# Two normalisations of a recurrence moved from VectorE to GpSimd, with one more pipeline stage and statistics kept for two tiles

## The chip, the cores and the metric

The kernel runs on one core of one Trainium2 chip. The core has TensorE (PE in the profile; its weight loads are PEld), VectorE (DVE), ScalarE (ACT), GpSimd (POOL) and SyncE (SP), which here issues DMAs. The metric is the time of one execution in device microseconds; lower is better.

## The reference

The input x is 2 x 1024 x 128 in float32. With `ln` a layer norm without gain, the program computes

```
x = x + 0.5 * F(ln(x))          # F: 6 layers of windowed attention and gated MLP
x = x + R(ln(x))                # R: a linear recurrence over time
x = x + 0.5 * F(ln(x))          # the same weights again

R(u):  h = u @ w_in.T + b_in
       s_t = sigmoid(a) * s_(t-1) + b * h_t      # per channel, along the 1024 positions
       return s @ w_out.T + b_out
```

Each layer of F projects to 16 heads of 64, normalises and rotates queries and keys, attends within windows of 32 and the window before, projects back and adds, then applies a gated MLP with a hidden width of 341. The change lies wholly in the middle: R, and the two layer norms around it.

## The kernel before, in words

The sequence is cut into 16 tiles of 128 positions (8 for each of the two sequences). 12 layers (6, and the same 6 again) times 16 tiles make 192 tile-layers. All engines run one software pipeline over them, fully unrolled: in step `s`, the stage with lag `L` works on tile-layer `s - L`. The stages of F have the lags 0 (transpose the input, project), 1 (keys, values, scores), 2 (softmax), 4 (attention output), 5 and 6 (MLP). Within a step, the order of each engine's instructions is simply the order of the code in its `step` function; engines meet at semaphores. The names used here:

- `proj`, `tps`, `sps`, `ops` are PSUM tensors that PE writes. `rot` (128x2048) holds rotated queries and keys, `swp` the other half of the rotation, `prob` the softmax, `hT` the hidden MLP values that PE multiplies at the end.
- `Z` holds the running activations of F, `xb` the residual x.

R is worked in between as further stages, active only for the 16 tiles between the 6th and the 7th layer. Their lags are named `M_...` and count from step 80 on:

- `M_X` = 7: DVE adds 0.5 Z to `xb` (L923), takes statistics (L938), aggregates them to mean and variance in `mmv[:, 0]` (L957) and adds the epsilon into `mrs` (L963). GpSimd raises that to the power -0.5 (L1138).
- `M_NORM` = 8: DVE normalises the tile into `mx_n` (L948), GpSimd adds the output bias `boB` to `xb` (L1142).
- `M_T` = 9: PE transposes `mx_n` (L650), ScalarE copies it out.
- `M_IN` = 10: PE multiplies by `winT` (L623), DVE adds bias and gain (L918) and runs the scan along time (L932, two inputs in SBUF: `siga` broadcast, and `mbh`).
- `M_OUT` = 11: PE multiplies by `woutT` (L626), DVE adds the result to `xb` (L914), takes its statistics (L928), aggregates (L953), adds the epsilon (L960); GpSimd takes the power (L1138).
- `M_Z` = 12: DVE normalises the tile into `Z` (L942), which the 7th layer reads: SP shifts it by DMA from stage 0 of tile-layer 96 on.

In DVE's `step`, `middle(k)` stands behind the last instruction of the reciprocal root (`rn`, L882) and ahead of `hT` (L1037), the row maximum `mx` (L1044) and the subtraction of it (L1047). On GpSimd a step is: a power on `rt` (L1114, the MLP's norm), the division of `prob` (L1118), two additions into `rot` (L1124), a small product for the tables (L1098), two multiplications of `rot` by `rn` (L1133, 128x1024 each, which wait for L882), then the middle's powers and the bias. A full step is one in which all these middle stages are active, a plain step one in which none is.

Of the kernel before, what the change touches and what calls it, by code (L numbers as in the profile page):

```python
# [17 lines left out]
ALU = mybir.AluOpType  # L18
# [3 lines left out]
P = 128  # L22
# [4 lines left out]
POS = SEQ // P  # L27
# [16 lines left out]


L_X, L_QKV, L_S, L_SM, L_AV, L_WO, L_F, L_F2 = 0, 1, 2, 3, 4, 4, 5, 6
M_X, M_NORM, M_T, M_IN, M_OUT, M_Z = 7, 8, 9, 10, 11, 12
FRONT = 6
UNROLL = 2
MID, MID_END = N - TILES + M_X - 1, N + M_Z  # L50
# [6 lines left out]
def macaron(nc, x_in, w_in, b_in, a_in, b_gain, w_out, b_out, w_qkv, q_scale, k_scale, w_o,  # L57
            ln_g, ln_b, w_1, b_1, w_2, b_2, c_rope, c_mask, c_ident, out):
    with ExitStack() as ctx:
# [7 lines left out]
        Z = sb("Z", [SLOTS * P])  # L67
# [47 lines left out]
        rawT = sb("rawT", [RAW])  # L115
        siga = sb("siga", [1])
        mst = sb("mst", [2, 6])
        mmv = sb("mmv", [2, 2])
        mrs = sb("mrs", [2])
        mx_n = sb("mx_n", [P])  # L120
        mx_t = sb("mx_t", [P])
        mbh = sb("mbh", [P])
# [694 lines left out]
        def _(dve):  # L817
# [90 lines left out]
            def middle(k):  # L908

                t = k.mid(M_OUT)  # L910
                if t is not None:
                    k.wait(p_f2, L_F2)
                    k.wait_mid(m_bo, M_OUT)
                    v.tensor_tensor(xb[:, t, :], xb[:, t, :], ops[:, 1, P:2 * P], ALU.add).then_inc(m_x2, 1)  # L914
                t = k.mid(M_IN)
                if t is not None:
                    k.wait(p_f2, L_F2)
                    v.tensor_scalar(mbh[:, :], ops[:, 1, 0:P], rawT[:, RAW_C:RAW_C + 1], rawT[:, RAW_C + 2:RAW_C + 3],  # L918
                                    ALU.add, ALU.mult).then_inc(m_bh, 1)
                t = k.mid(M_X)  # L920
                if t is not None:
                    k.wait(v_z, L_F2 + 1, base=TILES)
                    v.scalar_tensor_tensor(out=xb[:, t, :], in0=zslot(t), scalar=0.5, in1=xb[:, t, :],  # L923
                                           op0=ALU.mult, op1=ALU.add).then_inc(m_x1, 1)
                t = k.mid(M_OUT)
                if t is not None:
                    k.wait_mid(m_x2, M_OUT)
                    v.bn_stats(mst[:, 1, :], xb[:, t, :]).then_inc(m_st2, 1)  # L928
                t = k.mid(M_IN)
                if t is not None:  # L930
                    k.wait_mid(m_bh, M_IN)
                    v.tensor_tensor_scan(ys[:, t % 2, :], siga[:, :].to_broadcast([P, P]), mbh[:, :],  # L932
                                         0.0 if t % POS == 0 else ys[:, 1 - t % 2, P - 1:P],
                                         ALU.mult, ALU.add).then_inc(m_y, 1)
                t = k.mid(M_X)
                if t is not None:
                    k.wait_mid(m_x1, M_X)
                    v.bn_stats(mst[:, 0, :], xb[:, t, :]).then_inc(m_st, 1)  # L938
                t = k.mid(M_Z)
                if t is not None:  # L940
                    k.wait_mid(m_rs2, M_Z)
                    v.tensor_scalar(zslot(t), xb[:, t, :], mmv[:, 1, 0:1], mrs[:, 1:2],  # L942
                                    ALU.subtract, ALU.mult).then_inc(m_z, 1)
                t = k.mid(M_NORM)
                if t is not None:
                    k.wait(p_xT, L_X)
                    k.wait_mid(m_rs, M_NORM)
                    v.tensor_scalar(mx_n[:, :], xb[:, t, :], mmv[:, 0, 0:1], mrs[:, 0:1],  # L948
                                    ALU.subtract, ALU.mult).then_inc(m_xn, 1)
                if k.mid(M_OUT) is not None:  # L950
                    k.wait_mid(m_st2, M_OUT)
                    k.wait_mid(m_z, M_OUT + 1)
                    v.bn_aggr(mmv[:, 1, :], mst[:, 1, :]).then_inc(m_ag2, 1)  # L953
                if k.mid(M_X) is not None:
                    k.wait_mid(m_st, M_X)
                    k.wait_mid(m_xn, M_X + 1)
                    v.bn_aggr(mmv[:, 0, :], mst[:, 0, :]).then_inc(m_ag, 1)  # L957
                if k.mid(M_OUT) is not None:
                    k.wait_mid(m_ag2, M_OUT)
                    v.tensor_scalar(mrs[:, 1:2], mmv[:, 1, 1:2], 1e-5, None, ALU.add).then_inc(m_ve2, 1)  # L960
                if k.mid(M_X) is not None:
                    k.wait_mid(m_ag, M_X)
                    v.tensor_scalar(mrs[:, 0:1], mmv[:, 0, 1:2], 1e-5, None, ALU.add).then_inc(m_ve, 1)  # L963

            def step(k):
                if k.on(L_QKV):
# [126 lines left out]
        def _(pool):  # L1093
# [16 lines left out]
            def step(k):  # L1110
                if k.on(L_F):
                    k.wait(v_ve, L_F)
                    k.wait(a_xn, L_F + 1)
                    g_.tensor_tensor(rt2[:, 1:2], rt2[:, 0:1], half[:, 0:1], ALU.pow).then_inc(g_rstd, 1)  # L1114
                if k.on(L_SM):
                    k.wait(v_rec, L_SM)
                    pr = prob[:, :, :, :].rearrange("p a t j -> p (a t) j")
                    g_.tensor_tensor(pr, pr, rr[:, :].unsqueeze(2).to_broadcast([P, HEADS, 2 * WIN]),  # L1118
                                     ALU.mult).then_inc(g_nrm, 1)
                if k.on(L_QKV):  # L1120
                    for g in range(2):
                        k.wait(v_ab[1 + g], L_QKV)
                        r = rot[:, g * INNER:(g + 1) * INNER]
                        g_.tensor_tensor(r, r, swp[:, g * INNER:(g + 1) * INNER], ALU.add).then_inc(g_add[g], 1)  # L1124
                    src = k.off("rsrc", L_QKV, lambda u: (u % TILES) * (2 * DH))
                    dst = k.off("rdst", L_QKV, lambda u: ((u + TILES) % (2 * TILES)) * (2 * DH))
                    sc = k.off("rscl", L_QKV, lambda u: ((u // 4) % (4 * DEPTH)) * DH + 4 * DH)
                    tables(src, dst, sc)
                    k.wait(v_rs, L_QKV, per=RS_STEPS)
                    for g in range(2):  # L1130
                        k.wait(g_add[g], L_QKV)
                        r = heads(rot[:, g * INNER:(g + 1) * INNER])
                        g_.tensor_tensor(r, r, rn[:, g * HEADS:(g + 1) * HEADS].unsqueeze(2)  # L1133
                                         .to_broadcast([P, HEADS, DH]), ALU.mult).then_inc(g_nm[g], 1)
                for lag, n, ve, done in ((M_OUT, 1, m_ve2, m_rs2), (M_X, 0, m_ve, m_rs)):
                    if k.mid(lag) is not None:
                        k.wait_mid(ve, lag)
                        g_.tensor_tensor(mrs[:, n:n + 1], mrs[:, n:n + 1], half[:, 0:1], ALU.pow).then_inc(done, 1)  # L1138
                t = k.mid(M_NORM)
                if t is not None:  # L1140
                    k.wait_mid(m_xn, M_NORM)
                    g_.tensor_tensor(xb[:, t, :], xb[:, t, :], boB[:, :], ALU.add).then_inc(m_bo, 1)  # L1142

            def outer_pow(g):
                first, end = GROUPS[g]
# [87 lines left out]
```

## Time and profile before

| | |
|---|---|
| median of 3 runs | 3404.82 us (3398.56 to 3405.36) |
| the profiled execution, its own time | 3406.23 us |
| its span in the profile | 3404.4 us |
| mean granted TensorE clock | 0.992 |
| busy PE, DVE, ACT, POOL | 97%, 82%, 71%, 65% |
| shortest and longest L948 (128x128) | 1.673 and 2.012 us |
| shortest and longest L942 (128x128) | 0.331 and 1.857 us |

A busy time counts an instruction from its recorded start to its recorded end, so an instruction that is held by something after its start counts as busy. In the timeline, starts of neighbouring instructions on one engine can lie a little before the end of the one ahead. An idle time is put down to the instruction that ended it.

### The profile page before, as it was taken

The numbers are of one execution on the slowest core, as the hardware profiler recorded it, in microseconds if no ns is written. First come the engines' busy times: TensorE is split into PE (matmuls) and PEld (weight loads), VectorE is DVE, ScalarE is ACT, GpSimd is POOL, SyncE is SP. The second block draws the span as 40 slices with busy tenths as digits, with TensorE's granted clock in tenths as the row PEclk, the third lists the DMA queues.
The fourth block names the chain that finished last, engine by engine and source line by source line (L and its number), as shares of the span: only waits on it lengthen the run. The fifth ranks groups of instructions, "written<-read, shape, count | busy, mean of one in ns | idle before, by whom it ended". The sixth has DMA issues, their size and how long they took to land. (4 is left out here: it accounts for less than half of the span.)

```text
span 3404.4 us, 150755 instructions
## 1 busy us (share of the span) xinstructions
PE 3289.8 (97%) x63324; PEld 2485.3 (73%) x63515; DVE 2794.2 (82%) x6984; ACT 2426.8 (71%) x3769; POOL 2202.1 (65%) x1422
## 2 busy tenths in 40 slices
PE   6999999999999999999999999999999999999998
PEld 4777777777777777777667777777777777777776
DVE  5888888888888888889999888888888888888885
ACT  2777777777777777777667777777777777777775
POOL 4666666666666666666666666666666666666663
PEclk7999999999999999999999999999999999999998
DMA  3111111111111111111111111111111111111111
GB/s 114 51 47 51 48 51 48 50 48 47 51 47 51 48 50 48 51 48 45 46 41 46 51 48 51 48 51 44 48 48 51 48 51 48 51 48 50 50 51 42
DMA packets 199180, 170.06 MB, mean 50 GB/s; under 512 B 139610, under 2 KB 172525, under 8 KB 198509
## 3 DMA queue, kind: packets, MB, share of 16 engines
q1 hardware_dynamic: 193901, 157.05, 16.9%
q8 instruction: 509, 8.34, 1.0%
q10 hardware_dynamic: 4608, 3.34, 0.3%
q14 instruction: 162, 1.33, 0.1%
HBM read 33.38 MB, written 1.05 MB: 10 GB/s over the span
## 5 line engine op out<-in xcount | busy, mean ns | idle before, releaser
L1124 POOL TENSOR_TENSOR rot<-rot,swp 128x1024 f32<-128x1024 f32 x384 | 907.2, 2362 | 142.0 <-DVE rot L901 142.0
L705 ACT ACTIVATE sq<-proj 128x512 f32<-128x512 f32 x768 | 437.8, 596 | 573.5 <-PE proj L503 564.0
L503 PE MATMUL proj<-wq,xsT 128*128 128x512 f32 x1536 | 778.7, 627 | 30.0 <-DVE hT L1037 16.7
L1133 POOL TENSOR_TENSOR rot<-rot,rn 128x1024 f32<-128x1024 f32 x384 | 724.0, 1906 | 0.0
L1114 POOL TENSOR_TENSOR rt<-rt,half 128x1 f32<-128x1 f32 x192 | 105.3, 548 | 848.2 <-DVE rt L983 848.2
L895 DVE TENSOR_TENSOR swp<-proj,tab 128x512 f32<-128x512 f32 x768 | 522.1, 680 | 17.8 <-ACT sq L705 15.7
L901 DVE TENSOR_TENSOR rot<-proj,tab 128x512 f32<-128x512 f32 x768 | 519.0, 676 | 1.8 <-PE tps L514 1.8
L514 PEld LDWEIGHTS tps<-idf,rot 128*128 128x128 f32 x3072 | 361.6, 141 | 207.7 <-issue 203.5
L1037 DVE SCALAR_TENSOR_TENSOR hT<-proj,b1c,fg 114x128 f32<-114x128 f32 (+1 forms) x576 | 166.6, 345 | 413.5 <-ACT fg L769 407.3
L1118 POOL TENSOR_TENSOR prob<-prob,rr 128x1024 f32<-128x1024 f32 x192 | 365.4, 1903 | 187.3 <-DVE rr L995 187.3
L540 PEld LDWEIGHTS sps<-kT,qT 64*32 64x32 f32 x24576 | 365.5, 106 | 131.3 <-issue 130.9
L503 PEld LDWEIGHTS proj<-wq,xsT 128*128 128x128 f32 x1536 | 259.5, 190 | 255.4 <-issue 136.6
L540 PE MATMUL sps<-kT,qT 64*32 64x64 f32 x24576 | 407.5, 217 | 38.8 <-issue 38.7
L514 PE MATMUL tps<-idf,rot 128*128 128x128 f32 x3072 | 400.8, 274 | 3.2 <-POOL rot L1133 2.3
L509 PE MATMUL proj<-wq,xsT 128*128 128x512 f32 x768 | 386.1, 597 | 2.5 <-DVE rot L901 2.2
L555 PE MATMUL ops<-pT,vb 64*64 64x32 f32 x12288 | 378.8, 220 | 2.1 <-issue 2.1
L555 PE MATMUL ops<-pT,va 64*64 64x32 f32 x12288 | 375.8, 219 | 3.1 <-issue 2.9
L606 PE MATMUL ops<-wo,oT 128*128 128x128 f32 x3072 | 376.4, 276 | 2.4 <-ACT oT L727 2.4
L606 PEld LDWEIGHTS ops<-wo,oT 128*128 128x128 f32 x3072 | 359.8, 193 | 2.6 <-issue 2.6
L555 PEld LDWEIGHTS ops<-pT,vb 64*64 64x64 f32 x12288 | 329.4, 134 | 35.4 <-issue 34.7
L555 PEld LDWEIGHTS ops<-pT,va 64*64 64x64 f32 x12288 | 331.1, 135 | 4.0 <-issue 3.9
L522 PEld LDWEIGHTS proj<-xnT,w 128*114 128x114 f32 (+1 forms) x2304 | 264.3, 178 | 87.1 <-issue 81.7
(113 smaller groups left out, 5687.4 us busy)
## 6 DMA issues: line engine op xcount, KB each, us to landing
vb<-va SPq DMA_DIRECT2D x192, 384.0 KB, 3.5
vb<-va SPq DMA_DIRECT2D x192, 128.0 KB, 3.4
wq<-in_L_ffn_Wqkv SPq DMA_DIRECT2D x95, 192.0 KB
xs<-Z SPq DMA_DIRECT2D x384, 32.0 KB
xs<-Z SPq DMA_DIRECT2D x384, 28.0 KB
xs<-Z SPq DMA_DIRECT2D x384, 3.8 KB
xs<-Z SPq DMA_DIRECT2D x384, 0.2 KB
wo<-in_L_ffn_Wo SPq DMA_DIRECT2D x94, 64.0 KB
```

The lines of the kernel that those rows point to most:

```text
L503: mm(proj[:, c % 2, :], xsT[:, k.parity(L_QKV), :], wq2[:, bass.ds(w + c * 512, 512)], start=True, stop=True).then_inc(p_qkv[c], 1)
L509: mm(proj[:, c, :], xsT[:, k.parity(L_S), :], wq2[:, bass.ds(w + (4 + c) * 512, 512)], start=True, stop=True).then_inc(p_v[c], 1)
L514: last = tr(tps[:, p, :], rot[:, g * INNER + p * P:g * INNER + (p + 1) * P], idf[:, :])
L540: last = mm(sps[to:to + WIN, ty, p * 64:p * 64 + 64], qT[rows, p, w * WIN:(w + 1) * WIN], kT[rows, p, at:at + 2 * WIN], start=False, stop= ...
L555: last = mm(o4[hp * DH:(hp + 1) * DH, g, :], v, pT[rows, p, to:to + WIN], start=True, stop=True, skip_group_check=True)
L606: last = mm(ops[:, 0, 0:P], oT[:, p, :], wo[:, bass.ds(w + p * P, P)], start=(p == 0), stop=(p == PAIRS - 1))
L705: fn(sq[:, c * 512:(c + 1) * 512], proj[:, c % 2, :], ACT.Square).then_inc(a_sq[c], 1)
L895: v.tensor_tensor(halves(swp[:, c * 512:(c + 1) * 512]), swapped, tab[:, bass.ds(po + (2 * g + 1) * POS * DH, DH)] .rearrange("p (a d) -> ...
L901: v.tensor_tensor(heads(rot[:, c * 512:(c + 1) * 512]), heads(src), tab[:, bass.ds(po + 2 * g * POS * DH, DH)].unsqueeze(1) .to_broadcast( ...
L1118: g_.tensor_tensor(pr, pr, rr[:, :].unsqueeze(2).to_broadcast([P, HEADS, 2 * WIN]), ALU.mult).then_inc(g_nrm, 1)
L1124: g_.tensor_tensor(r, r, swp[:, g * INNER:(g + 1) * INNER], ALU.add).then_inc(g_add[g], 1)
L1133: g_.tensor_tensor(r, r, rn[:, g * HEADS:(g + 1) * HEADS].unsqueeze(2) .to_broadcast([P, HEADS, DH]), ALU.mult).then_inc(g_nm[g], 1)
```

## The change

- `M_Z` and `M_NORM` run on GpSimd, in a function `middle(k)` at the end of its step, behind the multiplications of `rot`.
- A new stage `M_ST` = 8 takes the statistics of the tile that `M_X` = 7 wrote a step before. `M_NORM`, `M_T`, `M_IN`, `M_OUT`, `M_Z` become 9, 10, 11, 12, 13.
- `mmv` and `mrs` have two slots, by the parity of the tile, so an aggregation waits for the reader of two tiles ago.
- On DVE, the statistics of `M_ST` stand ahead of those of `M_OUT`, and both ahead of the scan; before, the statistics of `M_X` stood behind it.
- The addition of `boB` goes from `M_NORM` to `M_T`; it and the two powers stand behind the two normalisations on GpSimd.

```diff
-M_X, M_NORM, M_T, M_IN, M_OUT, M_Z = 7, 8, 9, 10, 11, 12
+M_X, M_ST, M_NORM, M_T, M_IN, M_OUT, M_Z = 7, 8, 9, 10, 11, 12, 13
...
-        mmv = sb("mmv", [2, 2])
-        mrs = sb("mrs", [2])
+        mmv = sb("mmv", [2, 2, 2])
+        mrs = sb("mrs", [2, 2])
...
+                t = k.mid(M_ST)
+                if t is not None:
+                    k.wait_mid(m_x1, M_ST)
+                    v.bn_stats(mst[:, 0, :], xb[:, t, :]).then_inc(m_st, 1)
                 t = k.mid(M_OUT)
                 if t is not None:
                     k.wait_mid(m_x2, M_OUT)
...
-                t = k.mid(M_X)
-                if t is not None:
-                    k.wait_mid(m_x1, M_X)
-                    v.bn_stats(mst[:, 0, :], xb[:, t, :]).then_inc(m_st, 1)
-                t = k.mid(M_Z)
-                if t is not None:
-                    k.wait_mid(m_rs2, M_Z)
-                    v.tensor_scalar(zslot(t), xb[:, t, :], mmv[:, 1, 0:1], mrs[:, 1:2],
-                                    ALU.subtract, ALU.mult).then_inc(m_z, 1)
-                t = k.mid(M_NORM)
-                if t is not None:
-                    k.wait(p_xT, L_X)
-                    k.wait_mid(m_rs, M_NORM)
-                    v.tensor_scalar(mx_n[:, :], xb[:, t, :], mmv[:, 0, 0:1], mrs[:, 0:1],
-                                    ALU.subtract, ALU.mult).then_inc(m_xn, 1)
...
+                for n, lag, st_done, read, ag in ((0, M_ST, m_st, (m_xn, M_ST + 2), m_ag),
+                                                  (1, M_OUT, m_st2, (m_z, M_OUT + 2), m_ag2)):
+                    t = k.mid(lag)
+                    if t is not None:
+                        k.wait_mid(st_done, lag)
+                        k.wait_mid(*read)
+                        v.bn_aggr(mmv[:, n, t % 2, :], mst[:, n, :]).then_inc(ag, 1)
...
+            def middle(k):
+
+                t = k.mid(M_Z)
+                if t is not None:
+                    k.wait_mid(m_rs2, M_Z)
+                    g_.tensor_scalar(zslot(t), xb[:, t, :], mmv[:, 1, t % 2, 0:1], mrs[:, 1, t % 2:t % 2 + 1],
+                                     ALU.subtract, ALU.mult).then_inc(m_z, 1)
                 t = k.mid(M_NORM)
                 if t is not None:
-                    k.wait_mid(m_xn, M_NORM)
+                    k.wait(p_xT, L_X)
+                    k.wait_mid(m_rs, M_NORM)
+                    g_.tensor_scalar(mx_n[:, :], xb[:, t, :], mmv[:, 0, t % 2, 0:1], mrs[:, 0, t % 2:t % 2 + 1],
+                                     ALU.subtract, ALU.mult).then_inc(m_xn, 1)
+                t = k.mid(M_T)
+                if t is not None:
+                    k.wait_mid(m_xn, M_T)
                     g_.tensor_tensor(xb[:, t, :], xb[:, t, :], boB[:, :], ALU.add).then_inc(m_bo, 1)
```

On DVE a full step reads, between `rn` and `mx`, before (line, operation, output<-inputs, shape; the scan L932 is listed as SCALAR_TENSOR_TENSOR):

```order
L914 TENSOR_TENSOR xb<-xb,ops 128x128
L918 TENSOR_SCALAR mbh<-ops,rawT 128x128
L923 SCALAR_TENSOR_TENSOR xb<-Z,xb 128x128
L928 BN_STATS mst<-xb 128x6
L932 SCALAR_TENSOR_TENSOR ys<-siga,ys,mbh 128x128
L938 BN_STATS mst<-xb 128x6
L942 TENSOR_SCALAR Z<-xb,mmv,mrs 128x128
L948 TENSOR_SCALAR mx_n<-xb,mmv,mrs 128x128
L953 BN_AGGR mmv<-mst 128x2
L957 BN_AGGR mmv<-mst 128x2
L960 TENSOR_SCALAR mrs<-mmv 128x1
L963 TENSOR_SCALAR mrs<-mmv 128x1
```

and now (the scan is L936):

```order
L914 TENSOR_TENSOR xb<-xb,ops 128x128
L918 TENSOR_SCALAR mbh<-ops,rawT 128x128
L923 SCALAR_TENSOR_TENSOR xb<-Z,xb 128x128
L928 BN_STATS mst<-xb 128x6
L932 BN_STATS mst<-xb 128x6
L936 SCALAR_TENSOR_TENSOR ys<-siga,ys,mbh 128x128
L945 BN_AGGR mmv<-mst 128x2 x2
L950 TENSOR_SCALAR mrs<-mmv 128x1 x2
```

The two normalisations are gone, and the scan has moved behind the second statistics instruction.

On GpSimd a full step reads before, from the small table product on:

```order
L1098 TENSOR_TENSOR tab<-rope,scl 128x128
L1133 TENSOR_TENSOR rot<-rot,rn 128x1024 x2
L1138 TENSOR_TENSOR mrs<-mrs,half 128x1 x2
L1142 TENSOR_TENSOR xb<-xb,boB 128x128
L1114 TENSOR_TENSOR rt<-rt,half 128x1
```

and now:

```order
L1086 TENSOR_TENSOR tab<-rope,scl 128x128
L1121 TENSOR_TENSOR rot<-rot,rn 128x1024 x2
L1133 TENSOR_SCALAR Z<-xb,mmv,mrs 128x128
L1139 TENSOR_SCALAR mx_n<-xb,mmv,mrs 128x128
L1144 TENSOR_TENSOR xb<-xb,boB 128x128
L1150 TENSOR_TENSOR mrs<-mrs,half 128x1 x2
L1102 TENSOR_TENSOR rt<-rt,half 128x1
```

Two instructions of 128x128 have come in behind the multiplications of `rot`, and the powers went behind the bias.

## Rows read from the trace of the kernel before

**Rows 1.** The page's first part: busy us (share of the span) and instructions.

```profile
PE 3289.8 (97%) x63324; PEld 2485.3 (73%) x63515; DVE 2794.2 (82%) x6984; ACT 2426.8 (71%) x3769; POOL 2202.1 (65%) x1422
```

**Rows 2.** Windows: stretch, length; PE, PEld, DVE, ACT, POOL busy (instructions); clock; DMA.

```profile
1314.94:1520.28 205.34, 202.25 (x3949) 153.35 (x3962) 169.34 (x424) 151.25 (x234) 135.69 (x85) 1.00 0.18 49
1520.28:1590.72 70.44, 69.74 (x1327) 52.08 (x1331) 69.25 (x168) 50.93 (x81) 49.14 (x36) 1.00 0.18 48
1590.72:1805.50 214.78, 196.10 (x3675) 146.23 (x3685) 212.75 (x518) 141.31 (x227) 143.53 (x113) 1.00 0.16 44
1805.50:1825.14 19.64, 17.95 (x334) 13.29 (x335) 19.12 (x44) 12.58 (x20) 13.03 (x11) 1.00 0.13 36
1825.14:1860.36 35.22, 34.87 (x667) 26.48 (x669) 34.60 (x86) 24.79 (x39) 22.73 (x15) 1.00 0.18 48
1860.36:1894.59 34.23, 33.90 (x660) 25.70 (x662) 29.76 (x78) 25.21 (x39) 22.99 (x17) 1.00 0.18 49
```

**Rows 3.** Waits (total us, times, longest): two of the plain stretch, one of the full.

```profile
DVE hT L1037 <- ACT fg L769: 26.6, 12, 2.4
PE sps L540 <- issue: 2.5, 5, 1.0
...
PE proj L503 <- DVE hT L1037: 14.4, 10, 1.8
```

**Rows 4.** Timeline of DVE, a full step: start, duration, line, operation.

```profile
1648.51 0.87 DVE L1037 SCALAR_TENSOR_TENSOR hT<-proj,b1c,fg 114x128 f32<-114x128 f32 x3
...
1663.29 0.28 DVE L928 BATCH_NORM_STATS2 mst<-xb 128x6 f32<-128x128 f32 x1
1663.49 0.47 DVE L932 TENSOR_TENSOR_SCAN ys<-siga,ys,mbh 128x128 f32<-128x128 f32 x1
1663.88 0.26 DVE L938 BATCH_NORM_STATS2 mst<-xb 128x6 f32<-128x128 f32 x1
1664.07 1.67 DVE L942 TENSOR_SCALAR Z<-xb,mmv,mrs 128x128 f32<-128x128 f32 x1
1665.66 1.94 DVE L948 TENSOR_SCALAR mx_n<-xb,mmv,mrs 128x128 f32<-128x128 f32 x1
1667.52 0.17 DVE L953 BATCH_NORM_AGGREGATE mmv<-mst 128x2 f32<-128x6 f32 x1
...
1668.04 0.87 DVE L1037 SCALAR_TENSOR_TENSOR hT<-proj,b1c,fg 114x128 f32<-114x128 f32 x3
```

**Rows 5.** Timeline of POOL in the same step.

```profile
1654.56 0.55 POOL L1114 TENSOR_TENSOR rt<-rt,half 128x1 f32<-128x1 f32 x1 [4.59 <-DVE rt L983]
...
1663.18 0.50 POOL L1098 TENSOR_TENSOR tab<-rope,scl 128x128 f32<-128x128 f32 x1
1663.64 3.87 POOL L1133 TENSOR_TENSOR rot<-rot,rn 128x1024 f32<-128x1024 f32 x2
1668.00 1.06 POOL L1138 TENSOR_TENSOR mrs<-mrs,half 128x1 f32<-128x1 f32 x2 [0.48 <-DVE mrs L960]
1669.04 0.45 POOL L1142 TENSOR_TENSOR xb<-xb,boB 128x128 f32<-128x128 f32 x1
```

**Rows 6.** Timeline of DVE at the start: the first normalisation, with GpSimd idle.

```profile
4.64 0.35 DVE L837 TENSOR_SCALAR Z<-xb,mvo,rstd 128x128 f32<-128x128 f32 x1 [0.74 <-POOL rstd L1148]
```

**Rows 7.** Timelines of DVE and POOL in a step without scan, second of the recurrence.

```profile
1534.62 2.01 DVE L948 TENSOR_SCALAR mx_n<-xb,mmv,mrs 128x128 f32<-128x128 f32 x1
1536.95 0.15 DVE L963 TENSOR_SCALAR mrs<-mmv 128x1 f32<-128x1 f32 x1
...
1534.65 3.76 POOL L1133 TENSOR_TENSOR rot<-rot,rn 128x1024 f32<-128x1024 f32 x2
```

**Rows 8.** Timeline of PE in the full step: the recurrence's transposition and the next.

```profile
1661.91 0.27 PE L650 MATMUL tps<-idf,mx_n 128*128 128x128 f32 x1
1662.02 0.27 PE L652 MATMUL tps<-idf,xs 128*128 128x128 f32 x1
```

More of the change, by code:

```diff
@@ L944, in middle @@
-                t = k.mid(M_NORM)
-                if t is not None:
-                    k.wait(p_xT, L_X)
-                    k.wait_mid(m_rs, M_NORM)
-                    v.tensor_scalar(mx_n[:, :], xb[:, t, :], mmv[:, 0, 0:1], mrs[:, 0:1],
-                                    ALU.subtract, ALU.mult).then_inc(m_xn, 1)
[L950 to L963, printed above, removed]
+                for n, lag, st_done, read, ag in ((0, M_ST, m_st, (m_xn, M_ST + 2), m_ag),
[5 more added lines that the diff above has]
+                        v.bn_aggr(mmv[:, n, t % 2, :], mst[:, n, :]).then_inc(ag, 1)
@@ L965, in step @@
+                for n, lag, ag, ve in ((0, M_ST, m_ag, m_ve), (1, M_OUT, m_ag2, m_ve2)):
+                    t = k.mid(lag)
+                    if t is not None:
+                        k.wait_mid(ag, lag)
+                        v.tensor_scalar(mrs[:, n, t % 2:t % 2 + 1], mmv[:, n, t % 2, 1:2], 1e-5, None,
+                                        ALU.add).then_inc(ve, 1)
             def step(k):
@@ L1134, in step, with zslot @@
                                          .to_broadcast([P, HEADS, DH]), ALU.mult).then_inc(g_nm[g], 1)
[L1135 to L1138, printed above, removed]
+                middle(k)
+            def zslot(t):
+                return Z[:, (t + t // POS + 1) * P:(t + t // POS + 2) * P]
+            def middle(k):
[4 more added lines that the diff above has]
+                                     ALU.subtract, ALU.mult).then_inc(m_z, 1)
                 t = k.mid(M_NORM)
                 if t is not None:
-                    k.wait_mid(m_xn, M_NORM)
-                    g_.tensor_tensor(xb[:, t, :], xb[:, t, :], boB[:, :], ALU.add).then_inc(m_bo, 1)
+                    k.wait(p_xT, L_X)
[3 more added lines that the diff above has]
+                t = k.mid(M_T)
+                if t is not None:
+                    k.wait_mid(m_xn, M_T)
+                    g_.tensor_tensor(xb[:, t, :], xb[:, t, :], boB[:, :], ALU.add).then_inc(m_bo, 1)
+                for lag, n, ve, done in ((M_OUT, 1, m_ve2, m_rs2), (M_ST, 0, m_ve, m_rs)):
+                    t = k.mid(lag)
+                    if t is not None:
+                        k.wait_mid(ve, lag)
+                        r = mrs[:, n, t % 2:t % 2 + 1]
+                        g_.tensor_tensor(r, r, half[:, 0:1], ALU.pow).then_inc(done, 1)
             def outer_pow(g):
```

## The prediction

> **What bounds the kernel now.** I read the page's summary first. TensorE (PE) is busy 97% of the span, VectorE (DVE) 82%, GpSimd (POOL) 65% [rows 1]. That says "PE", but it is an average over nearly 200 steps of one software pipeline, and the change touches only some 20 steps in the middle. So the second view is the table of stretches, cut where the row maximum (`mx`, L1044) of successive steps starts [rows 2]. Twelve plain steps take 205.34 us, 17.11 each. The 11 steps in which every part of the recurrence is active take 214.78 us, 19.53 each. In the plain stretch DVE is busy 169.34 of 205.34 us; in the full one 212.75 of 214.78. The recurrence's steps are bound by DVE, and PE has slack there.
>
> The waits say the same [rows 3]. In plain steps DVE sits before `hT` for ScalarE's `fg` (26.6 us in 12 steps); in full steps DVE never waits for an engine and PE waits for `hT` (14.4 us over 10 recorded waits, up to 1.8 each). Plain steps also hold irregular PE pauses of up to 1.0 us without a releaser (5 in 12 steps), part of the 17.11.
>
> Then one full step in the timeline [rows 4, 5]. Two DVE instructions stick out: the normalisation into `Z` (L942, 1.67 us) and the one into `mx_n` (L948, 1.94 us). The same work takes 0.35 us at the start of the kernel when GpSimd is idle [rows 6]. Their ends tell why they are long: GpSimd's two multiplications of `rot` (L1133) run from 1663.64 to 1667.51, half each, so the first ends near 1665.5 and the second at 1667.51. L942 ends at 1665.74, L948 at 1667.60. Each was held until the GpSimd instruction beside it was done. Nearly all of their 3.61 us is waiting for GpSimd, not work.
>
> **What the change removes.** L942 and L948 leave DVE. From L942's start (1664.07) to L953's start (1667.52) is 3.45 us per full step [rows 4]. If nothing took their place, DVE's step would be 19.53 - 3.45 = 16.08, less than PE needs. PE's own need is 17.11 plus the recurrence's five matmul instructions (two for each of the two projections, one transposition), at 0.11 each, the spacing of L650 and L652 [rows 8]: 17.66.
>
> **What it moves, and why the gain is smaller on DVE.** The new order puts the statistics of `x1` ahead of those of `x2`, and both ahead of the scan. The scan therefore starts one statistics instruction later, 0.20 us (L928 to L932, 1663.29 to 1663.49) [rows 4]. That matters. Does a scan contend with GpSimd? The rows say so from GpSimd's side: in the step with the scan the two multiplications take 3.87 us [rows 5], in one without it 3.76 [rows 7]; the scan, which starts 0.15 us ahead of them while the table product L1098 still runs, gets in between and costs them 0.11. Against that, L948 in the early step starts at 1534.62, 0.03 ahead of the multiplication at 1534.65, and is held the whole 2.01 us [rows 7]. So the race is lost somewhere between 0.15 and 0.03 us of lead. The moved scan would start at 1663.69, 0.05 *behind* the multiplication at 1663.64. I expect it to be held until the first multiplication ends.
>
> The Trainium skill (SBUF — State Buffer, "Who interferes with whom") has the same rule: a VectorE instruction with two SBUF inputs contends with a GpSimd instruction that reads SBUF, and the loser blocks for the whole instruction. By that rule the scan blocks; 3.87 against 3.76 agrees.
>
> Worked out for a full step: the second multiplication would start at 1663.64 + 1.88 = 1665.52. The scan today ends 0.32 us after a multiplication's start (1663.96 against 1663.64), so it would end at 1665.84 and the next instruction start 0.08 earlier, as L938 does, at 1665.76. From L953 to `hT` is 0.52 (1667.52 to 1668.04), so `hT` starts at 1666.28. The last `hT` was at 1648.51: a step of 17.77 us, against 19.53. That is just above PE's 17.66, so either engine's irregular pauses are now partly seen; I add 0.13 and take 17.9.
>
> The small instructions that follow (two aggregations, two additions of one element) now run while the second multiplication does. Are they held? No: L963 took 0.15 us at 1536.95, inside GpSimd's 1534.65 to 1538.41 [rows 7], and 0.15 when GpSimd was idle. They stay at nothing.
>
> **What it adds on GpSimd.** Two 128x128 `tensor_scalar` per full step. The trace has none on GpSimd. Nearest by size is the 128x128 addition L1142, 0.45 us; above it the 128x1024 multiplication, 1.9 us for eight times the elements [rows 5]; below nothing is not to be had. I take 0.45 each. Do they hide? GpSimd's next step begins with the power of `rt` (L1114), which it awaits from DVE: at 1654.56, 6.05 us behind the `hT` at 1648.51. In the new step the multiplications start 2.64 us ahead of `hT` and take 3.87; then come 2c for the two new ones, 0.45 and 1.06 (L1142, L1138). GpSimd is free at 2.74 + 2c behind `hT`, against 6.05: c may be 1.65 us before anyone waits. At 0.45 there is 2.4 us to spare; at 1.9 it is missed by 0.5, some 5 us in all. The second new instruction also brings a wait to GpSimd, for PE's transposition of `xs` (L652): that started at 1662.02, over 5 us before GpSimd gets there, so the powers queued behind it lose nothing.
>
> **The added stage and the double statistics** cost no step: the pipeline's length stays. They give each result a step of distance. The DMA queue (SP) issues nothing new; it waits for `z` of a tile at the step L_X, four steps behind the old writing and three behind the new one. On GpSimd the addition of `boB` and the two powers now stand behind the normalisations; PE's transposition and DVE's additions want them a step later. The statistics move off the value written just ahead of them, worth a few hundredths of a microsecond beside other waits. All taken as nothing.
>
> **The sum** by stretches [rows 2]:
> - first four steps, 70.44 us (one held normalisation in each): new 4 x 17.11 plus PE's extras of 0.44 = 68.88, -1.6
> - 11 full steps, 214.78: new 11 x 17.9 = 196.9, -17.9
> - the step at 1805.50, 19.64: the scan is 0.28 earlier without `x1`'s addition and wins its race, new 17.66, -2.0
> - the next two, 35.22, now PE-bound at 17.66: +0.1
> - the last two, 34.23, with one stage more still active: 17.55 + 17.33, +0.65
>
> Together -20.7, say -21. The profiled execution took 3406.2 us (its span 3404.4): 3385. It lies 1.4 above the median of the runs shown, 3404.8, so the median should be 3384.
>
> **The rivals.**
> - *The scan is not held* (the race is won, or lost by less): DVE's step is 16.1 and PE bounds at 17.66. Full steps give -20.6, in all -23.4; where the irregular pauses vanish too, 0.2 to 0.3 a step more, -27. About 3381, down to 3378. For it: the race is within 0.1 us. Against: L948. Chance 0.15.
> - *The hold passes on in full*: the scan, once held, is not let in between the two multiplications but behind both. Then it ends near 1667.7, the step is about 19.6 and only the edges gain: -2, 3403. The Trainium skill (Perfetto Trace Analysis, "Optimizing Scalar/DVE Operations") warns that since GpSimd and VectorE share a port, offloading between them might not help; this would be that case. Against it: L942 did get in between in every full step. Chance 0.08.
> - *GpSimd becomes the bound* (the slower side): each new instruction costs c, more than 1.65, and the step becomes 17.77 + 2c - 3.3. The gain of a full step is gone at c = 2.5. At c = 3, half more than the 128x1024 multiplication, it is 20.5, 0.95 longer than before in the 10 steps that hold both, 0.8 and 2.7 longer in the two behind them, with -1.6 from the first of the 11 full steps (only one of the two runs there) and -0.9 from the edges left: +10.5, 3415. For it: no such instruction in the trace, and operands given per partition. Against: 3 is nearly seven times the 128x128 row. Chance 0.03.
> - The forecast keeps 0.74.
>
> The Trainium skill (GPSIMD Engine Reference, "Instruction dispatch") gives about 6 us for the first call of a freshly loaded GpSimd kernel. By it the sum would be some 4 us smaller, once; the trace shows no such gap where GpSimd changes from copies to products.
>
> **How the numbers follow.** A measurement of this kernel tells about 0.2% from no change, 6.8 us. Faster by more: the forecast, the first rival, nearly all: 0.90. Within, mainly the second rival: 0.07. Slower: 0.03. The range reaches below to the first rival's 3378, above to GpSimd at its upper bound (+5, 3389), and 3 and 5 us beyond, because the three runs shown lie 7 us apart: 3375 to 3394. The second and third rival stay outside.
>
> **What would show it.** Steps of 17.6 to 18.0 us from the first full step on. A scan (L936) of about 2.1 us in 11 steps that ends 0.3 behind the first multiplication's end, 0.5 to 0.7 in the others. `hT` still not waiting for ScalarE in full steps. PE's wait for `hT` down from 1.8 to a few tenths. GpSimd's new instructions near 0.45 us, with 2 to 3 us of idle time ahead of the power that begins its next step. Scans of 0.5 us everywhere would be the first rival; steps of 19.5 with scans of 4 us the second; GpSimd without idle time ahead of the power the third.

## The result and the profile after

Over four runs each, the changed kernel takes 3377.97 us in the median (3377.11 to 3380.69) and the one before 3401.69 us (3397.75 to 3405.36): a ratio of 0.9925, with a 95% interval of 0.9913 to 0.9938. It is 24 us faster. The forecast was 3384, the range 3375 to 3394. Two executions of experiments, of 8,369 and 11,475 us on one chip, are left out below; in the one of them that was profiled, TensorE was slow throughout (a projection instruction, L503, took 1,411 ns in the mean, against 627 in the kernel before).

The page's first part of the changed kernel, against [rows 1]:

```profile
PE 3288.9 (97%) x63515; PEld 2482.8 (73%) x63515; DVE 2758.7 (82%) x6952; ACT 2424.5 (72%) x3769; POOL 2227.0 (66%) x1454
```

VectorE has lost 35.5 us of busy time, GpSimd has gained 24.9. The span fell by 25.5 us (3404.4 to 3378.9). The windows of the changed kernel, cut at the same steps as [rows 2] (first four of the recurrence, 11 full ones, one, two, two; columns as there):

```profile
1521.26:1589.58 68.32, 67.75 (x1325) 51.67 (x1326) 61.51 (x158) 50.71 (x80) 48.36 (x35) 1.00 0.18 49
1589.58:1785.36 195.78, 191.88 (x3686) 146.56 (x3686) 192.11 (x495) 140.57 (x226) 157.82 (x130) 1.00 0.18 48
1785.36:1802.57 17.21, 17.13 (x335) 13.19 (x335) 15.66 (x44) 12.56 (x20) 13.77 (x13) 1.00 0.16 42
1802.57:1837.91 35.34, 34.99 (x671) 26.97 (x672) 31.21 (x83) 25.53 (x41) 28.57 (x24) 1.00 0.18 48
1837.91:1873.05 35.14, 34.60 (x667) 26.34 (x668) 30.37 (x81) 25.19 (x39) 25.29 (x20) 1.00 0.18 48
```

The 11 full steps went from 214.78 to 195.78 us, 19.53 to 17.80 each. The 20 steps together went from 374.31 to 351.79, 22.5 us less; the other 3.0 of the 25.5 lie outside them, nearly all of it code that has not changed.

A full step of the changed kernel in VectorE's timeline, against [rows 4]:

```profile
1638.98 0.27 DVE L932 BATCH_NORM_STATS2 mst<-xb 128x6 f32<-128x128 f32 x1
1639.18 2.13 DVE L936 TENSOR_TENSOR_SCAN ys<-siga,ys,mbh 128x128 f32<-128x128 f32 x1
1641.23 0.21 DVE L945 BATCH_NORM_AGGREGATE mmv<-mst 128x2 f32<-128x6 f32 x2
1641.42 0.22 DVE L950 TENSOR_SCALAR mrs<-mmv 128x1 f32<-128x1 f32 x2
1641.60 0.87 DVE L1025 SCALAR_TENSOR_TENSOR hT<-proj,b1c,fg 114x128 f32<-114x128 f32 x3
```

and in GpSimd's, against [rows 5]:

```profile
1639.13 3.87 POOL L1121 TENSOR_TENSOR rot<-rot,rn 128x1024 f32<-128x1024 f32 x2
1643.00 0.79 POOL L1133 TENSOR_SCALAR Z<-xb,mmv,mrs 128x128 f32<-128x128 f32 x1
1643.78 0.79 POOL L1139 TENSOR_SCALAR mx_n<-xb,mmv,mrs 128x128 f32<-128x128 f32 x1
1644.54 0.46 POOL L1144 TENSOR_TENSOR xb<-xb,boB 128x128 f32<-128x128 f32 x1
1644.95 1.08 POOL L1150 TENSOR_TENSOR mrs<-mrs,half 128x1 f32<-128x1 f32 x2
1647.65 0.55 POOL L1102 TENSOR_TENSOR rt<-rt,half 128x1 f32<-128x1 f32 x1 [1.62 <-DVE rt L971]
```

The reader is to see three things. The scan starts 0.05 us behind the multiplication (1639.18 against 1639.13) and takes 2.13 us instead of 0.47; this happens in all 11 full steps, from 1603.98 to 1781.88, and in none of the five others that have a scan, where it starts 0.15 to 0.38 ahead of the multiplication and takes 0.47 to 0.71. A normalisation on GpSimd costs 0.79 us, not 0.45. And there is still idle time (1.62 us) ahead of the power that opens GpSimd's next step.

The waits in the full steps changed with that. Waits of TensorE's weight loads for `hT` (total us, times, longest) before (1590.72 to 1805.50), and then in the changed kernel (1589.58 to 1785.36):

```profile
PEld proj L503 <- DVE hT L1037: 23.3, 11, 2.7
...
PEld proj L503 <- DVE hT L1025: 3.3, 8, 0.7
```

TensorE's matmuls no longer wait for `hT` there at all, and VectorE waits for another engine in two of the 11 steps only, for the scores (1.5 us together): it still sets the step in most of them.

### The profile page after: what moved, and what is told of

Same layout as the page of the kernel before. It is cut to its first block and busy times, and to the rows that moved or that the text cites. A ratio compares the mean times of both kernels' runs of the same rounds, so it can differ in the third digit from the quotient of the medians.

```text
span 3378.9 us, 150942 instructions
## 1 busy us (share of the span) xinstructions
PE 3288.9 (97%) x63515; PEld 2482.8 (73%) x63515; DVE 2758.7 (82%) x6952; ACT 2424.5 (72%) x3769; POOL 2227.0 (66%) x1454
## 3 DMA queue, kind: packets, MB, share of 16 engines
q14 instruction: 162, 1.33, 0.1%
## 5 line engine op out<-in xcount | busy, mean ns | idle before, releaser
L503 PE MATMUL proj<-wq,xsT 128*128 128x512 f32 x1536 | 772.4, 625 | 14.4 <-DVE rot L901 10.2
L503 PEld LDWEIGHTS proj<-wq,xsT 128*128 128x128 f32 x1536 | 261.0, 190 | 232.3 <-issue 139.3
L1032 DVE TENSOR_REDUCE mx<-sps 128x16 f32<-128x1024 f32 x192 | 235.1, 1224 | 114.7 <-PE sps L540 111.0
## 6 DMA issues: line engine op xcount, KB each, us to landing
vb<-va SPq DMA_DIRECT2D x192, 384.0 KB, 3.5
```

The lines of the kernel that those rows point to most:

```text
L503: mm(proj[:, c % 2, :], xsT[:, k.parity(L_QKV), :], wq2[:, bass.ds(w + c * 512, 512)], start=True, stop=True).then_inc(p_qkv[c], 1)
```

## The experiments

Each kernel was run beside the kernel before on the same chip. Scan first, no stage, late on VectorE and on VectorE shared one chip (the kernel before: 3401.5 us in the median). The other seven ran on another chip, in two groups: move only, twice and three times (before: 3398.9), and the four marked "again" (before: 3403.5). So rows of different groups are compared by their ratios. The table gives, from each kernel's profiled execution, the mean of the 11 full steps and the sum of the 22 steps from the first with `M_X` to the last with `M_Z` of the longer pipeline. The full steps are the last 11 in which both `M_X` and the output stage (`M_OUT`) run, cut at `mx` as in [rows 2]; with the old lags a twelfth lies ahead of them and is not counted.

| kernel | median us (n) | ratio to before, 95% | full step, us | 22 steps, us | rest of the span, us |
|---|---|---|---|---|---|
| before | 3401.7 (4) | | 19.53 | 408.7 | 2995.7 |
| changed | 3378.0 (4) | 0.9925 (0.9913 to 0.9938) | 17.80 | 386.6 | 2992.3 |
| changed, again | 3379.8 (5) | 0.9931 (0.9920 to 0.9943) | 17.75 | 386.7 | 2992.0 |
| scan first | 3375.7 (5) | 0.9921 (0.9907 to 0.9936) | 17.44 | 383.4 | 2989.2 |
| scan first, again | 3376.0 (5) | 0.9920 (0.9908 to 0.9932) | 17.50 | 384.0 | 2990.2 |
| no stage | 3381.1 (4) | 0.9935 (0.9922 to 0.9949) | 17.63 | 384.8 | 2994.8 |
| no stage, again | 3379.9 (5) | 0.9926 (0.9913 to 0.9939) | 17.58 | 383.5 | 2994.6 |
| late on VectorE | 3380.0 (4) | 0.9931 (0.9918 to 0.9945) | - | - | - |
| late on VectorE, again | 3382.0 (6) | 0.9940 (0.9926 to 0.9954) | 17.82 | 386.4 | 2993.4 |
| on VectorE | 3409.0 (11) | 1.0018 (1.0009 to 1.0026) | 19.85 | 415.5 | 2988.9 |
| move only | 3447.2 (4) | 1.0134 (1.0118 to 1.0151) | 21.87 | 460.0 | 2987.5 |
| twice | 3375.1 (4) | 0.9929 (0.9915 to 0.9944) | 17.71 | 386.0 | 2992.6 |
| three times | 3386.5 (4) | 0.9962 (0.9948 to 0.9977) | 18.49 | 396.8 | 2987.6 |

The last column is code that no kernel changes. It moves by 8 us between the profiled executions of different kernels, so times of whole kernels that lie 3 or 4 us apart say little unless they are measured side by side, and the steps say more. In the three kernels that were profiled twice it came out alike, within 0.3, 1.0 and 0.2 us. Whether it moves by chance or goes with the kernel is therefore open.

### The scan ahead of the statistics

```diff
...
-                t = k.mid(M_ST)
-                if t is not None:
-                    k.wait_mid(m_x1, M_ST)
-                    v.bn_stats(mst[:, 0, :], xb[:, t, :]).then_inc(m_st, 1)
                 t = k.mid(M_OUT)
...
                                          0.0 if t % POS == 0 else ys[:, 1 - t % 2, P - 1:P],
                                          ALU.mult, ALU.add).then_inc(m_y, 1)
+                t = k.mid(M_ST)
+                if t is not None:
+                    k.wait_mid(m_x1, M_ST)
+                    v.bn_stats(mst[:, 0, :], xb[:, t, :]).then_inc(m_st, 1)
```

> The changed kernel, with one edit: the scan stands ahead of the statistics of M_ST again, so that it starts about 0.2 us earlier. Theory A (the scan loses a race by 0.05 us and is then held by the first multiplication): the scan takes 0.47 us in all 11 full steps instead of 2.13, VectorE's full step shrinks to about 16 us, and TensorE sets the step: 17.35 us in a step without a pause (16.80 + 5 x 0.11), 17.66 in the mean with pauses. The changed kernel's full steps are 17.80 in the mean, so the gain is small: 1.5 us (0 to 5), about 3376 us. Theory B (VectorE is still the one bound of the full steps): the whole 1.7 us of the hold comes off each of 11 steps, 18 us, 3360.

Measured: 3375.7 us. Timelines of a full step (from the repetition below), VectorE and then GpSimd:

```profile
1635.58 0.47 DVE L932 TENSOR_TENSOR_SCAN ys<-siga,ys,mbh 128x128 f32<-128x128 f32 x1
1635.97 0.26 DVE L938 BATCH_NORM_STATS2 mst<-xb 128x6 f32<-128x128 f32 x1
...
1637.50 0.87 DVE L1025 SCALAR_TENSOR_TENSOR hT<-proj,b1c,fg 114x128 f32<-114x128 f32 x3 [0.58 <-ACT fg L769]
1638.65 1.23 DVE L1032 TENSOR_REDUCE mx<-sps 128x16 f32<-128x1024 f32 x1 [0.28 <-PE sps L540]
...
1635.73 3.88 POOL L1121 TENSOR_TENSOR rot<-rot,rn 128x1024 f32<-128x1024 f32 x2
```

0.15 us ahead of the multiplication instead of 0.05 behind it, the scan takes 0.47 us. That shows the race. VectorE's waits in the full steps (total us, times, longest), first of the changed kernel, then of this one:

```profile
DVE mx L1032 <- PE sps L540: 1.5, 2, 0.9
...
DVE hT L1025 <- ACT fg L769: 7.6, 11, 0.8
DVE mx L1032 <- PE sps L540: 4.9, 10, 1.4
```

VectorE now waits in every full step, for ScalarE and mostly for the scores too, as in a plain one: it is no longer the bound. So only a little of the 1.66 us per scan came off the time, as theory A says. The shortest full steps are 17.17 us, below the 17.35 I had worked out. The expectation for theory B, 3360 us, is far off.

The same pair side by side:

> The changed kernel once more, on the chip of the next three runs. On record it is 22.0 us shorter in the 22 steps of the recurrence and 3.5 us outside them, where nothing changed. Theory A (the 3.5 us are TensorE's irregular pauses, which fall differently in each execution): the median is 3375 to 3382 us, and the middle of the profiled execution is 22 us (21 to 24) shorter than before's.

> The changed kernel with the scan ahead of the statistics of M_ST, measured beside the changed kernel itself. The first look gave full steps of 17.44 us in the mean against 17.80, 4.0 us over 11 of them. Theory A: 3 to 5 us faster than the changed kernel on the same chip. Rival (TensorE's pauses swallow it): within 1.5 us.

3379.8 us (3378.3 to 3381.5) against 3376.0 (3374.7 to 3378.0): 3.8 us, and the runs do not overlap. Of that, 2.8 us lie in the 11 full steps (195.30 against 192.48 us). Theory A holds for both; the middle of the changed kernel is 22.0 us shorter than before's again. The reason given for the 3.5 us outside it, pauses that fall differently in each execution, is not borne out: that part is 2992.0 us, as it was (2992.3).

### The same normalisations on VectorE, where GpSimd is idle

Against the kernel before, besides the slots:

```diff
-                t = k.mid(M_Z)
-                if t is not None:
-                    k.wait_mid(m_rs2, M_Z)
-                    v.tensor_scalar(zslot(t), xb[:, t, :], mmv[:, 1, 0:1], mrs[:, 1:2],
-                                    ALU.subtract, ALU.mult).then_inc(m_z, 1)
...
                 if k.on(L_WO):
                     k.wait(d_xs2, L_WO, per=64)
                     v.bn_stats(st[:, :], xs2[:, :]).then_inc(v_bn, 1)
+                t = k.mid(M_Z)
+                if t is not None:
+                    k.wait_mid(m_rs2, M_Z)
+                    v.tensor_scalar(zslot(t), xb[:, t, :], mmv[:, 1, t % 2, 0:1], mrs[:, 1, t % 2:t % 2 + 1],
+                                    ALU.subtract, ALU.mult).then_inc(m_z, 1)
...
```

and the same for `M_NORM` and `mx_n`.

> The kernel before, with the two normalisations still on VectorE, but at the end of its step (behind the statistics st of the MLP's norm), where GpSimd is idle, and mmv and mrs in two slots. Old lags, scan where it was. Theory A (each normalisation costs 0.35 us and the rest was the hold by GpSimd's multiplication): both take 0.33 to 0.40 us, VectorE's full step is 16.7 us, TensorE sets it at 17.4 to 17.7, and the time is 3376 us, like the changed kernel, with no work moved to another engine. Rival (the instructions are long because of their per-partition operands, or VectorE simply has too much work): they stay above 1 us each, full steps stay near 19 us, 3395 or more.

Four executions gave a median of 3380.0 us; the fifth, the profiled one, is the one of 8,369 us. The same kernel again:

> The normalisations on VectorE at the end of its step, where GpSimd is idle; in the first attempt the profiled execution was unusable, because TensorE ran at a fraction of its speed in all of it. Theory A: both instructions take 0.33 to 0.40 us, full steps of 17.2 us without a pause, 17.4 to 17.7 in the mean, and the time is that of the kernel with the scan first, within 3 us. Rival: they stay above 1 us each.

Timelines of a full step of the repetition, VectorE and GpSimd:

```profile
1645.87 0.33 DVE L1044 TENSOR_SCALAR Z<-xb,mmv,mrs 128x128 f32<-128x128 f32 x1
1646.11 0.34 DVE L1050 TENSOR_SCALAR mx_n<-xb,mmv,mrs 128x128 f32<-128x128 f32 x1
...
1640.65 3.88 POOL L1132 TENSOR_TENSOR rot<-rot,rn 128x1024 f32<-128x1024 f32 x2
1644.49 1.06 POOL L1139 TENSOR_TENSOR mrs<-mrs,half 128x1 f32<-128x1 f32 x2
```

Over all tiles they take 0.329 to 0.345 us. The same instructions on the same engine took 1.67 and 1.94 us while GpSimd multiplied. This settles what the long durations were, and 21 us of the gain are to be had without moving any work to another engine. The second slots are in this kernel too; whether it needs them was not run. The time missed its expectation: it is 6 us above the kernel with the scan first, not within 3. Of these, 3.5 us are in the full steps, 17.82 us in the mean and not below 17.37. In the first full step (18.13 us) the scan starts 0.31 us behind the multiplication and takes 1.92 us. For the rest, the waits of TensorE's weight loads in the full steps point to a cause, first this kernel's, then that of the scan first, again (total us, times, longest):

```profile
PEld proj L503 <- DVE rot L901: 8.1, 12, 1.0
```

```profile
PEld proj L503 <- DVE rot L901: 2.8, 11, 0.3
```

The place at the end of VectorE's step lies directly ahead of the rotations, which TensorE's next projection waits for. By these waits 0.5 us of work there is late for TensorE. That is argued; no run moves the two instructions elsewhere in VectorE's idle stretch.

### The stage and the slots without the other engine

The changed kernel with both normalisations back in VectorE's `middle`, behind the scan:

```diff
                                          ALU.mult, ALU.add).then_inc(m_y, 1)
+                t = k.mid(M_Z)
+                if t is not None:
+                    k.wait_mid(m_rs2, M_Z)
+                    v.tensor_scalar(zslot(t), xb[:, t, :], mmv[:, 1, t % 2, 0:1], mrs[:, 1, t % 2:t % 2 + 1],
+                                    ALU.subtract, ALU.mult).then_inc(m_z, 1)
...
-                    g_.tensor_scalar(zslot(t), xb[:, t, :], mmv[:, 1, t % 2, 0:1], mrs[:, 1, t % 2:t % 2 + 1],
-                                     ALU.subtract, ALU.mult).then_inc(m_z, 1)
...
```

> The changed kernel with its stage, lags, slots and order, but the two normalisations back on VectorE, behind the scan. Theory A: three instructions contend now. The scan is held until the first multiplication ends, the normalisation into Z until the second ends, the one into mx_n perhaps behind GpSimd's addition of the bias: full steps of 19.5 to 20.0 us, 3400 to 3409 us, no gain over the kernel before. Rival (the stage and the two slots bring the gain, not the other engine): full steps near 17.8, 3378.

Measured: 3409.0 us, ratio 1.0018. Timelines of a full step, VectorE and GpSimd:

```profile
1643.22 1.72 DVE L936 TENSOR_TENSOR_SCAN ys<-siga,ys,mbh 128x128 f32<-128x128 f32 x1
1644.87 1.86 DVE L942 TENSOR_SCALAR Z<-xb,mmv,mrs 128x128 f32<-128x128 f32 x1
1646.64 0.49 DVE L948 TENSOR_SCALAR mx_n<-xb,mmv,mrs 128x128 f32<-128x128 f32 x1
...
1642.70 3.94 POOL L1132 TENSOR_TENSOR rot<-rot,rn 128x1024 f32<-128x1024 f32 x2
1646.60 0.45 POOL L1144 TENSOR_TENSOR xb<-xb,boB 128x128 f32<-128x128 f32 x1
```

The scan ends 0.3 us behind the middle of the multiplications (1644.94), the normalisation into `Z` at their end (1646.73 against 1646.64), and the one into `mx_n` is held a little by the bias: nine of the 11 full steps are 19.8 us long. Theory A; the stage and the slots by themselves bring nothing here. The steps are 0.3 us longer than before: the moved scan is held now (1.7 to 2.1 us), and with it a third instruction contends.

### The move without the second slot

Against the kernel before, with `mmv` and `mrs` as they were; the same for `mx_n`:

```diff
-                    v.tensor_scalar(zslot(t), xb[:, t, :], mmv[:, 1, 0:1], mrs[:, 1:2],
-                                    ALU.subtract, ALU.mult).then_inc(m_z, 1)
...
+                t = k.mid(M_Z)
+                if t is not None:
+                    k.wait_mid(m_rs2, M_Z)
+                    g_.tensor_scalar(zslot(t), xb[:, t, :], mmv[:, 1, 0:1], mrs[:, 1:2],
+                                    ALU.subtract, ALU.mult).then_inc(m_z, 1)
...
                 for lag, n, ve, done in ((M_OUT, 1, m_ve2, m_rs2), (M_X, 0, m_ve, m_rs)):
```

> The kernel before, with the two normalisations moved to GpSimd and nothing else: one slot of statistics, old lags. VectorE's aggregations now wait in the same step for GpSimd's normalisations (m_z, m_xn), which stand behind the two multiplications. Theory A (two slots are what makes the move pay): hT follows the second multiplication by 2 x 0.79 + 0.45 us, 1.5 later than before, full steps of 21 us; steps with one normalisation lose 2 to 2.6 us each; 35 us in all, 3437 us (3420 to 3445). Rival (the slots cost and bring nothing): 3378.

Measured: 3447.2 us, 48 us slower than before, and 2 us above the upper end of what was expected. VectorE and GpSimd in a full step:

```profile
1616.10 0.26 DVE L938 BATCH_NORM_STATS2 mst<-xb 128x6 f32<-128x128 f32 x1
1618.76 0.18 DVE L942 BATCH_NORM_AGGREGATE mmv<-mst 128x2 f32<-128x6 f32 x1 [2.40 <-POOL Z L1127]
1619.54 0.18 DVE L946 BATCH_NORM_AGGREGATE mmv<-mst 128x2 f32<-128x6 f32 x1 [0.60 <-POOL mx_n L1133]
...
1617.86 0.80 POOL L1127 TENSOR_SCALAR Z<-xb,mmv,mrs 128x128 f32<-128x128 f32 x1
1618.64 0.79 POOL L1133 TENSOR_SCALAR mx_n<-xb,mmv,mrs 128x128 f32<-128x128 f32 x1
```

The hold has become a semaphore wait, and it is longer: with one slot, VectorE may not aggregate before GpSimd has read the last statistics. The shortest full step is 21.00 us, as expected. So the slots are what makes the move pay (the next experiment differs from this one in them alone). The rest, 10 us over 11 full steps (21.87 in the mean), has another cause: six of them take 21.00 us, and the other five, at a lower granted clock (0.81 to 0.93), hold all of it. Two successive windows:

```profile
1599.66:1620.66 21.00, 17.75 (x334) 13.17 (x335) 17.71 (x47) 12.97 (x21) 14.51 (x13) 0.98 0.17 46
1620.66:1645.17 24.51, 21.71 (x334) 16.19 (x335) 16.28 (x47) 12.67 (x20) 14.51 (x13) 0.81 0.10 28
```

The granted clock of the longer one is 0.81. At its beginning TensorE has sat idle for 3.20 us waiting for `hT`; then a pair of projection instructions takes 2.07 us, against 1.12 in the step before, which is the lower level, 1.2 GHz. Each of the four waits of 3.2 us for `hT` in the full steps opens one of the five slow steps, though the clock can fall some instructions behind it: at 1666.31 the pair still takes 1.13 us, and the step is 23.34 us long, at a clock of 0.85. After a wait of 2.77 us at 1689.64 the pair takes 1.12 and the step 21.00. The Trainium skill (Perfetto Trace Analysis, "Matmul Optimizations") says that TensorE's power follows its use and asks for matmuls back to back; these two windows agree.

### The move and the slots without the stage

The edit of the last experiment, and with it the two slots; the statistics of x1 stay in `M_X`, behind the scan.

```diff
-        mmv = sb("mmv", [2, 2])
-        mrs = sb("mrs", [2])
+        mmv = sb("mmv", [2, 2, 2])
+        mrs = sb("mrs", [2, 2])
...
+                for n, lag, st_done, read, ag in ((1, M_OUT, m_st2, (m_z, M_OUT + 2), m_ag2),
+                                                  (0, M_X, m_st, (m_xn, M_X + 2), m_ag)):
...
```

> The kernel before, with the two normalisations on GpSimd behind the multiplications and mmv and mrs in two slots, but without the added stage: the statistics of x1 stay in M_X behind the scan, the old lags stay. Theory A (the gain is the hold that leaves VectorE; the stage itself brings nothing): full steps of 17.4 to 17.7 us bound by TensorE, scans of 0.47 us, 3375 us, the same as the kernel with the scan first, within 3 us. Rival (the added stage is needed to hide the statistics or the power): VectorE or GpSimd waits in each full step and the time lies 5 us or more above the changed kernel's.

> Normalisations on GpSimd and two slots, without the added stage. In the first look it was 5.7 us slower than the kernel with the scan first, but only 1.4 us of that lay in the steps of the recurrence. Theory A (the stage brings at most 1.5 us, the rest were pauses elsewhere): within 3 us of the kernel with the scan first. Rival (the stage is worth its 5 us): 5 to 6 us slower again.

Measured: 3381.1 and 3379.9 us, 5.4 and 3.9 us above the scan-first kernel measured beside it, outside the 3 us expected (in the second pair the runs overlap: 3373.4 to 3380.3 against 3374.7 to 3378.0). But the 22 steps take 384.8 and 383.5 us, against 383.4 and 384.0: within the recurrence the stage is worth nothing that can be seen. The scans were not all of 0.47 us, as expected: in three of the 11 full steps, both times, the scan starts 0.3 us behind the multiplication and takes 1.92 us; what makes it late there is not shown. The difference between the kernels lies in the last column of the table, in code that is the same: 5.6 and 4.4 us. Its cause stays open.

### How much GpSimd can take

In the changed kernel, each normalisation two and three times (the additional results go to a buffer `mdm` that nobody reads). For twice, and likewise for `mx_n`:

```diff
                     k.wait_mid(m_rs2, M_Z)
+                    g_.tensor_scalar(mdm[:, 0, :], xb[:, t, :], mmv[:, 1, t % 2, 0:1], mrs[:, 1, t % 2:t % 2 + 1],
+                                     ALU.subtract, ALU.mult)
                     g_.tensor_scalar(zslot(t), xb[:, t, :], mmv[:, 1, t % 2, 0:1], mrs[:, 1, t % 2:t % 2 + 1],
                                      ALU.subtract, ALU.mult).then_inc(m_z, 1)
```

> The changed kernel, with each of GpSimd's normalisations done twice (the extra results go to a buffer nobody reads): 2 x 0.79 = 1.58 us more on GpSimd per full step. The changed kernel has 1.62 us of idle time ahead of the power L1102 in a full step. Theory A (GpSimd's work there is covered up to that idle time): no change, 3378 us within 3, idle time ahead of that power 0 to 0.1. Rival (GpSimd's accesses slow VectorE or are on the path already): 1 us or more per full step, 3390 or more.

> The changed kernel, with each of GpSimd's normalisations done three times: 3.16 us more on GpSimd per full step, 1.5 beyond its idle time. Theory A: the step grows by 1.1 to 1.5 us in the 12 steps that hold both, 19 us each, 12 to 17 us in all, 3390 to 3395 us. Rival (the power on rt is not what VectorE waits for, so GpSimd may be late without harm): 3378 to 3381.

Twice: 3375.1 us, by its ratio (0.9929) the same as the changed kernel (0.9925 and 0.9931), full steps without a pause 17.60 us as in the changed kernel, and no idle time ahead of the power:

```profile
1645.21 1.08 POOL L1155 TENSOR_TENSOR mrs<-mrs,half 128x1 f32<-128x1 f32 x2
1646.34 0.55 POOL L1103 TENSOR_TENSOR rt<-rt,half 128x1 f32<-128x1 f32 x1
```

Three times: 3386.5 us. The steps that hold both normalisations take 18.68 us, 1.08 longer; VectorE's waits in them have a new entry (total us, times, longest):

```profile
DVE nb L980 <- POOL rt L1103: 7.5, 8, 1.0
```

1.58 us of work more cost nothing, 3.16 cost 1.08. The first matches the 1.62 us of idle time; of the 1.54 beyond it, 0.46 do not show in the step. The size of the total was missed: 10.2 us in the 22 steps (396.8 against 386.6), where I had expected 12 to 17; the time lies 3.5 us below the 3390 expected.

## Why the prediction was right

**The bound of the full steps** was VectorE, as read. It never waited in them before, and TensorE's waits for `hT` are gone with the hold (its weight loads', 23.3 us, are down to 3.3). With the scan first, which takes the last hold away, VectorE begins to wait.

**What made the two instructions long** was the hold by GpSimd. 0.33 and 0.34 us where GpSimd is idle, against 1.67 and 1.94, show it.

**The moved scan** loses its race and is held once: forecast 2.1 us in 11 steps, measured 2.13 in 11 steps. The first rival fell; the second (held behind both) fell too, since the scan ends 0.3 us behind the first multiplication. The race was read a little too generally: "lost somewhere between 0.15 and 0.03 us of lead" comes from a normalisation, and a scan in the move-only kernel that starts 0.02 us ahead (1877.01 against 1877.03) takes 0.47 us. The forecast did not hang on it, since its scan starts behind.

**VectorE's full step** was forecast at 17.77 us and is 17.60 where no pause falls. The term that was off is the tail from the scan to `hT`, taken as 0.52 us from [rows 4]: it measures 0.37 (1641.23 to 1641.60), because aggregations and additions now come in pairs, without waits on the instruction just ahead. The 0.13 added for pauses should have been 0.20 (17.80 in the mean).

**The cost on GpSimd** was off by 0.34 us each: 0.79, not 0.45. It changed nothing, since it was hidden, and it is far from the third rival's 1.65 and more; the idle time forecast at 2 to 3 us shrank to 1.62. That cover was real: the limit worked out as c = 1.65 us per instruction has the measured one between 0.79 x 2 = 1.58 (nothing lost) and 0.79 x 3 = 2.37 (1.08 us lost).

**The sum** by stretches came out at -2.1, -19.0, -2.4, +0.1 and +0.9, against -1.6, -17.9, -2.0, +0.1 and +0.65. Together -22.5 against -20.7. The remaining 3 us of the span's 25.5 lie outside the recurrence, where the profiled executions of all these kernels differ by up to 8 us; their cause is open. The forecast of the time, 3384, was 6 us high: 3.1 of these come from its base, the median of three runs before (3404.8; with the fourth it is 3401.7), and 2.9 from the size of the change (23.7, not 20.8).

**TensorE's need** of 17.66 us in the mean was a little high: with the scan first the full steps are 17.44 and 17.50 us, shortest 17.17.

**The added stage at nothing** agrees with the no-stage kernels in the 22 steps. The slots were taken at nothing too; that was right for the change as it stands, but the reason given was thin: without them the move costs 48 us.

## What to carry to other kernels

An instruction whose duration changes with what GpSimd is doing is waiting, not working: compare its end with the ends of GpSimd's instructions, and look for the same instruction in a stretch where GpSimd is idle. Moving it helps as far as its successors don't inherit the hold and no buffer ties the engines together in the same step; here 0.2 us in the start of the scan decided the first, a second slot the second. Where the engine has a stretch beside an idle GpSimd, leaving the instruction there brought nearly as much (21 of 24 us). When an engine stops being the bound, further savings on it are worth almost nothing: 1.66 us per step off the scan gave 0.3.

## What the runs showed of the hardware

- The race between the two engines is settled by a few hundredths of a microsecond. Scans that started 0.15 us ahead of a multiplication got through in 0.47 us in all kernels, as did one 0.02 ahead (move only, 1877.01); those 0.03 to 0.05 us behind took 2.13 or 2.14. For a `tensor_scalar` the border lies elsewhere: 0.03 ahead lost (2.01 us, [rows 7]), 0.15 ahead got through (0.32 us, on VectorE, 1550.90).
- Scans that started 0.35 to 0.40 us ahead took 0.67 to 0.72 us and ended where those 0.15 ahead did, 0.3 us behind the multiplication's start. GpSimd's table product ran beside them (in the changed kernel 1834.31 to 1834.78, the scan 1834.36 to 1835.06): by these numbers it holds them too.
- Aggregations and one-element additions aren't held: in the full steps of the changed kernel they took 0.14 to 0.16 us each beside GpSimd's multiplication. A `tensor_scalar` of 128x6 was: 1.33 us at 28.60 in the kernel before, beside the multiplications that start at 28.01, and 0.17 us at 51.29.
- GpSimd's `tensor_scalar` of 128x128 takes 0.79 us with two operands given per partition, its addition of two 128x128 tensors 0.45: fewer tensor inputs, but longer. No gap appears ahead of the first of them, at 1556.24.
- Each of the four waits of 3.2 us on TensorE in the move-only kernel was followed, in the same step, by a stretch at the lower clock level (1.2 GHz): granted clocks of 0.81 to 0.91 and steps 0.8 to 3.5 us above 21.00. One of the waits of 2.5 to 2.8 us in the full steps was followed by it as well (0.93, 0.6 us), four were not.
